# Adding the attention mask in the instruction that takes the row maxima

## What is computed

```
scores = jnp.einsum('bhqd,bhkd->bhqk', query, key_) / jnp.sqrt(jnp.asarray(D_K, query.dtype))
scores = jnp.where(mask == 0, jnp.asarray(NEG, scores.dtype), scores)
attn = jax.nn.softmax(scores, axis=-1)
ctx = jnp.einsum('bhqk,bhkd->bhqd', attn, value)
```

## Time and profile before

| | us |
|---|---|
| median of three runs | 436.0 |
| the profiled execution | 434.68 |
| its span | 432.9 |
| busy: PE / DVE / ACT / POOL | 359.2 / 242.1 / 151.1 / 56.6 |

### The profile page before, as it was taken

One profiled execution on the slowest core, in us unless ns is written; L12 is line 12 of the kernel. 1 busy time (PEld: TensorE's weight loads), 2 busy tenths in 40 slices (PEclk: granted clock), 3 DMA queues, 4 the chain that ended last, 5 costly groups with the idle time before them and its releaser, 6 DMA issues.

```text
span 432.9 us, 6018 instructions
## 1 busy us (share of the span) xinstructions
PE 359.2 (83%) x2063; PEld 247.6 (57%) x2063; DVE 242.1 (56%) x682; ACT 151.1 (35%) x300; POOL 56.6 (13%) x85
## 2 busy tenths in 40 slices
PE   1455168749987799779997799999989999999996
PEld 0343136433454535464454445988878888788875
DVE  2373568672297833963279541757567645554553
ACT  3504413705734166005541374223233222222221
POOL 7322131642012130001000200010000000000000
PEclk9866687766997999957899599989999999999999
DMA  4201284601005110151000003000000000000000
GB/s 113 59 12 34 58 197 136 145 6 46 0 2 129 26 44 2 37 115 45 2 0 2 5 2 97 2 0 2 1 26 0 0 26 2 0 2 24 0 0 24
DMA packets 17296, 15.38 MB, mean 36 GB/s; under 512 B 4469, under 2 KB 16693, under 8 KB 16981
## 3 DMA queue, kind: packets, MB, share of 16 engines
q1 hardware_dynamic: 16885, 14.84, 13.6%
q10 hardware_dynamic: 384, 0.20, 0.2%
HBM read 11.72 MB, written 3.11 MB: 34 GB/s over the span
## 4 chain that ended last, share of the span: by engine, by line
PE 69%; DVE 14%; ACT 5%; DMA 5%; issue 3%; ACTq 1%; POOL 1%; SPq 0%; DVEq 0%; POOLq 0%
PE pS L1056 14%; DVE nmax_mask L908 5%; PE pS L1205 5%; PE pS L1202 4%; PE pC L1220 4%; PE pS L253 4%; PE pS L255 3%; PE pS L254 3%; PE pC L1217 3%; PE pA L253 3%; PE pA L254 3%; PE pA L255 3%; PE pB L253 3%; PE pB L255 3%; PE pB L254 3%
## 5 line engine op out<-in xcount | busy, mean ns | idle before, releaser
L1056 PEld LDWEIGHTS pS<-prob,sig 128*128 128x128 f32 x512 | 65.4, 192 | 13.7 <-DVE res L720 6.3
L709 DVE TENSOR_TENSOR sig<-xi_f,pS 128x512 f32<-128x512 f32 x64 | 43.9, 685 | 50.9 <-PE pS L255 46.0
L1056 PE MATMUL pS<-prob,sig 128*128 128x128 f32 x512 | 69.6, 280 | 1.2 <-DVE sig L709 1.0
L908 DVE TENSOR_REDUCE nmax_mask<-pS 128x3 f32<-128x462 f32 (+1 forms) x96 | 52.5, 574 | 12.8 <-PE pS L1178 12.1
L636 ACT ACTIVATE prob<-pS 128x512 f32<-128x512 f32 x80 | 43.9, 597 | 31.7 <-PE pS L1205 31.7
L1175 PE MATMUL pS<-k_stack,q_stack 72*128 72x154 bf16 x256 | 36.8, 251 | 13.3 <-DVE nmax_mask L908 10.2
L720 DVE SCALAR_TENSOR_TENSOR res<-pS,w_gate,res 128x128 f32<-128x128 f32 (+1 forms) x128 | 36.0, 344 | 14.3 <-PE pS L1056 13.4
L553 ACT ACTIVATE xi_f<-pA 128x512 f32<-128x512 f32 x32 | 19.1, 598 | 61.4 <-PE pA L255 61.3
L1175 PEld LDWEIGHTS pS<-k_stack,q_stack 72*128 72x128 bf16 x256 | 21.2, 106 | 32.8 <-DVE nmax_mask L908 23.3
L553 ACT ACTIVATE xi_f<-pB 128x512 f32<-128x512 f32 x32 | 19.1, 598 | 52.5 <-PE pB L255 52.4
L1178 PE MATMUL pS<-mbias,ident_bf 128*128 128x462 bf16 (+1 forms) x96 | 36.4, 380 | 0.0
(11 more groups left out here) (275 smaller groups left out, 647.8 us busy)
## 6 DMA issues: line engine op xcount, KB each, us to landing
q_stack<-q_scr SPq DMA_DIRECT2D x12, 384.0 KB
q_scr<-q_parts SPq DMA_DIRECT2D x12, 128.0 KB, 2.3
k_stack<-k_scr SPq DMA_DIRECT2D x36, 40.0 KB
res<-in_x_dram SPq DMA_DIRECT2D x4, 256.0 KB, 6.3
prob<-in_L_ffn_wg_dram SPq DMA_DIRECT2D x1, 1024.0 KB, 5.9
prob<-in_L_ffn_wp_dram SPq DMA_DIRECT2D x1, 1024.0 KB, 9.6
out_dram<-res SPq DMA_DIRECT2D x4, 256.0 KB, 2.2
prob<-in_L_ffn_wo_dram SPq DMA_DIRECT2D x1, 768.0 KB, 5.0
```

Of the source, the lines that this page charges most:

```text
L709: dve.tensor_tensor(hid[:, i % 2, :], relu[:, i % 2, :], pUp[i % 2][:, :], ALU.mult).then_inc(s_hid, 1)
L908: dve.tensor_reduce(nmax[:, qt, hs[0]:hs[-1] + 1], score_bank(b, n)[:, 0:len(hs) * KEYS].rearrange("p (h k) -> p h k", k=KEYS), AX.X, ALU. ...
L1056: last = pe.matmul(pO[:, toks], hid[:, i % 2, toks], wo_sb[:, e, hf, :], start=(hf == 0 and t == 0), stop=(hf == HF - 1), skip_group_check ...
```

## The change

The identity product is gone: the last score product of a unit closes the accumulation and signals VectorE. VectorE takes one instruction a head in place of one a unit: it adds `mbias` of that query tile to the head's 154 scores, multiplies by -1, writes the result back over the scores in PSUM, and takes the minimum into `nmax`. The value is the same negated maximum. What is written back is read by nobody.

```
                 elif step == "scores_max":
                     qt, hs = SA_UNITS[n]
                     dve.wait_ge(s_sa, NSA * b + n + 1)
-                    dve.tensor_reduce(nmax[:, qt, hs[0]:hs[-1] + 1],
-                                      score_bank(b, n)[:, 0:len(hs) * KEYS].rearrange("p (h k) -> p h k", k=KEYS),
-                                      AX.X, ALU.max, negate=True).then_inc(s_red, 1)
+                    for i, h in enumerate(hs):
+                        cols = score_bank(b, n)[:, i * KEYS:(i + 1) * KEYS]
+                        last = dve.tensor_tensor_reduce(out=cols, in0=cols, in1=mbias[:, qt, :], scale=-1.0,
+                                                        scalar=F32_MAX, op0=ALU.add, op1=ALU.min,
+                                                        accum_out=nmax[:, qt, h:h + 1])
+                    last.then_inc(s_red, 1)
...
                     for i, h in enumerate(hs):
-                        pe.matmul(dst[:, i * KEYS:(i + 1) * KEYS], q_stack[b % 2][0:STACK, h, qt * P:(qt + 1) * P],
-                                  k_stack[b % 2][0:STACK, h, 0:KEYS], start=(i == 0), stop=False,
-                                  skip_group_check=True)
-                    pe.matmul(dst[:, 0:len(hs) * KEYS].rearrange("p (h k) -> p h k", k=KEYS), ident_bf[:, :],
-                              mbias[:, qt, :].unsqueeze(1).broadcast_to([P, len(hs), KEYS]),
-                              start=False, stop=True, skip_group_check=True).then_inc(s_sa, 1)
+                        last = pe.matmul(dst[:, i * KEYS:(i + 1) * KEYS],
+                                         q_stack[b % 2][0:STACK, h, qt * P:(qt + 1) * P],
+                                         k_stack[b % 2][0:STACK, h, 0:KEYS], start=(i == 0), stop=True,
+                                         skip_group_check=True)
+                    last.then_inc(s_sa, 1)
```

## The result

The changed kernel takes **449.6 us** (median of four executions, 448.3 to 451.8), the kernel before 435.7 beside it. The ratio is 1.034 (95% interval 1.027 to 1.041): slower by 14 us, where 22 were forecast. A second series of six executions gave 451.4 and a ratio of 1.035 (1.030 to 1.040).

A forecast was written before the change was run, and what follows sets the result against it. VectorE was taken to bound the score-maxima stages. Batches of +3.3, +4.2, +5.7 and +7.3 (20.5 us) and +2 for the clock, on 434.7, gave 457.2; as a median 458 us, range 449 to 484.

The forecast's parts named there:

- What bounds the kernel: Middle of the four score-maxima stages: VectorE full, each us added to its queue adds time, TensorE's saving worth nothing.
- The cost of a head: VectorE, per head: fused instruction 0.23 us plus accumulator read 0.09, together 0.32; ends 0.23 and 0.46.
- the main instruction: VectorE's fused instruction over a head's 154 scores: 0.23 us to the next start, upper end 0.31.
- the read: Second VectorE instruction of each head, writing the accumulated value: 0.09 us, bounded between zero and 0.15.
- the forecast's own: VectorE at 0.29 to 0.36 us a head, with both ends of the clock: 449 to 470 us, chance 62%.
- (b): VectorE's accumulator read is covered: up to 0.28 us a head, 440 us; chance 8%.
- Stage by stage: Score-maxima stages, extra VectorE work less idle time: batches 0 to 3 +3.3, +4.2, +5.7, +7.3, sum 20.5 us.
- the tail: End of batch 1's maxima, where TensorE bounds: identity products gone save 1.1 us, last unit costs 0.25, so -0.85.
- The clock: TensorE, less busy, opens score stages at half clock, at most +2.9 us in batch 1: +2, ends -1 and +5.
- (a): On VectorE each instruction waits for the one before: 0.46 us a head; chance 25%, including 0.37 to 0.50.
- (c): TensorE's saving decides the stages, a head costing 0.18 to 0.20 us on VectorE: 433 us; chance 3%.
- What would show it: Profile after: VectorE busy up 30 to 60 us from 242, heads 0.32 apart, TensorE's waits for the maxima grown.

The follow-up runs named there:

- the changed tail: Kernel before with fused maxima and no mask product only in the last four units of batches 0 and 1: 438.0 us, ratio 1.002.

## Why the prediction was right in its kind and 8 us too high

**What bounds the kernel**: right. VectorE was the full engine in the stages and stayed so, and TensorE's saving was worth nothing where it is full.

**The cost of a head**: the term that was mis-sized. Forecast 0.23 for the main instruction and 0.09 for the read, 0.32. The main one was right to a hundredth: 0.235, for the first head of a unit. The read cost nothing, but a head behind a head cost 0.04 more, since the output goes to PSUM (0.235 with it in SBUF). On average some 0.27. Both ends had been bounded from neighbouring rows, and the 0.09 was taken between zero and 0.15 with nothing to decide it. The prediction's own working says 2.0 us per 0.01 us a head (20.5 at 0.32, 16.5 at 0.30); at 0.27 it gives 20.5 - 5 x 2.0 = 10.5, and 11.2 was measured. The time still came out inside the range, which was luck in part: 0.27 lies outside the forecast's own 0.29 to 0.36 and in what was given 8% with rival (b), and 449.6 is 0.6 us above the range's lower end.

**Stage by stage** (forecast, measured): batch 0 +3.3, +1.3; batch 1 +4.2, +2.1; batch 2 +5.7, +3.5; batch 3 +7.3, +4.4. The order is as forecast, batches with more idle time before absorbing more. The terms of the forecast don't add up quite to these figures (batch 2's, 0.66 + 6.0 - 0.8, make 5.9, and batch 0's first step 0.53 for 0.65), but the slips are under 0.2 us each. In batch 1, from the first maxima: unit 7 +0.65 (forecast +1.4), the second act_lo three units later +1.4 (forecast +1.4 and 3 x 0.41, +2.6), the second xi_f +3.0 (forecast +5.0), the split +2.1, so the tail gave back 0.9 (forecast 0.85): every step of the full stretch is too high by the cost of a head, and the tail is right. In the tail VectorE still waits for TensorE, in the timeline of the changed kernel:

```profile
143.61 0.33 DVE L911 CUSTOM_DVE_ANT_0 pS<-pS,mbias 128x154 f32<-128x154 f32 x1 [1.74 <-PE pS L1179]
...
146.13 0.33 DVE L911 CUSTOM_DVE_ANT_0 pS<-pS,mbias 128x154 f32<-128x154 f32 x1 [0.21 <-PE pS L1179]
```

**The clock**: right in sum by luck, wrong in place. Forecast +2; the gaps came out 2.5 longer in the profiled execution and 4.4 in the second series. The forecast had it mostly behind batch 1, with 1 us each behind batches 2 and 3. Behind the last split, batch 3's, it is 3.3 in both, and the gaps behind batches 1 and 2 are no longer than before. Batch 1's score stage was to open at 0.50, and opened at full clock, with products 0.22 us apart:

```profile
152.60 0.39 PE L1208 MATMUL pS<-mbiasT_rem,ident_bf 128*128 128x512 bf16 x1
152.82 0.38 PE L1205 MATMUL pS<-q_stack,k_stack 75*128 75x512 bf16 x1
```

The slower stretches are in batches 2 and 3 (granted 0.50 from 183 to 206 us, before from 183 to 200; and from 234 to 261, before 237 to 247) and in two short stretches among the experts (before, one). Read in windows of 2 us (one at 0.75 counts as half at 0.50), TensorE stood at 0.50 for 65 of the 190 us from 60 to 250 before, and for 88 after. The prediction took the clock for a side effect of 1 us here and there. The runs showed that neither saving on TensorE brought time (1.003 and 1.002) and that spare products were worth 4.7 us. That it is the clock which takes the savings back fits these profiles, and is argued from them: no run kept the clock up and left out the products with a clear result.

**The rivals.** (a), each instruction waiting for the one before, would have shown heads 0.46 apart: they are 0.235 to 0.275 apart, with rows of 347 ns. What the Trainium skill says in "The DRAIN you can't avoid" (VectorE: DVE Perf Modes), that the next operation can't be issued before the pipe is empty, doesn't hold for this sequence; the section itself adds that a next operation which isn't held starts earlier, and the starts agree with that. The rule of "Two Vector instructions with no wait between them" on the same page (an accumulator read is an instruction of its own, not held if its output starts in the same quadrant as the last one into that memory) agrees with the trace. It says nothing of the 0.04 us that the write to PSUM adds. (b), the read covered, was right in its mechanism, and its 440 too low because it took +0.14 a unit of three where 0.24 to 0.275 came. (c) needed 0.21 us a head. Even a plain reduction of one head takes 0.227, so none of the forms run here, with an instruction a head, meets its condition, and the kernel without the product shows that there was nothing to win: 436.4.

**What would show it**: VectorE's busy time rose by 22, below the 30 to 60 said, for the same reason as the sum. The TensorE waits grew as said.

## What to carry to other kernels

Before fusing an operation into another engine's instruction, ask what it does to the number of instructions there: here the 3-head reduction had to be cut into heads, which alone made up about half of the stages' loss (its share of the time is less clear), and the work taken over came from an engine that was waiting. If a fused instruction with an accumulator has a result that nobody reads, send it to SBUF, not over its operand in PSUM: 445.1 for 451.4 us. And a saving on TensorE that leaves it idle for longer has to be checked against its granted clock. Here 96 products fewer brought nothing (436.4 us), and a few spare ones into a free bank brought 4.7 us (431.7).

## What the runs showed of the hardware

- A fused add, scale and minimum over 154 f32 of PSUM and 154 bf16 of SBUF, with an accumulator output, starts 0.235 us after the one before with its result in SBUF (f32 or bf16 alike, 311 ns long), and 0.275 with its result written over its operand in PSUM (347 ns). The separate accumulator read is hidden in both, and its row is 81 ns in the first and 139 in the second.
- A plain reduction of 154 f32 of PSUM starts 0.227 us after its like; of 308, 0.39; of 462, 0.55. By the last two 154 elements cost 0.16, which leaves some 0.07 for the fixed part of an instruction, an estimate from these starts.
- Right after the last head of batch 0 the four small operations of the split last 1.1 to 1.2 us each, where in batch 1 they last 0.2. Timeline of VectorE, changed kernel, the first two of them:

```profile
89.82 1.11 DVE L920 CAST m_parts<-nmax_mask 128x64 bf16<-128x64 f32 x1
90.97 1.22 DVE L922 TENSOR_TENSOR m_r<-nmax_mask,m_parts 128x64 f32<-128x64 f32 x1
```

GpSimd is at work at that place (until 94.5 us), and not in batch 1. In the kernel before GpSimd's work ends at 91.9 us, and the fourth operation, at 91.96, lasts 0.23 again. The cause wasn't tested.
- Executions of one kernel differ by over 1%, at different granted clocks: with the changed tail from 434.7 us to 441.3, at means of 0.866 to 0.900. That is more than most of the effects sought here. In the kernel with the changed tail and spare products the two go together, in all six executions, from 427.8 us at 0.927 to 437.7 at 0.885. But without mask products 430.1 us and 438.4 came at 0.867 and 0.866, so the mean clock isn't all that differs; no profile shows the second kind.
